# Expert inputs by one-hot tables on TensorE in place of scatters through memory, and another order of modulation, norms and z products in the front

## The chip, the cores and the metric

The kernel runs on one core of a Trainium2 chip. The metric is the device time of one execution in microseconds. A core has TensorE (PE in the profile, with its weight loads as PEld), VectorE (DVE), ScalarE (ACT), GpSimd (POOL) and SyncE (SP); they run side by side, each takes its own instructions in order, and they meet at semaphores. SP and POOL issue DMAs, which all share 16 DMA engines.

## The reference, cut to what matters

Two layers on 1024 tokens of width 256. In each, a conditioning vector c gives six rows (shift, scale and gate for the mixer and for the feed-forward part). Layer 0 is a Mamba-like mixer (SSD) and a mixture of 64 experts, top 8, with room for 64 tokens each; layer 1 is sliding-window attention and a dense feed-forward part with 4-bit weights.

```python
mod = silu(c) @ wmod                      # six rows of 256 per layer
# layer 0, mixer
proj = u_n @ in_proj_w.T                  # z 512, x 512, B 128, C 128, dt 8
B, C = rms_norm(B), rms_norm(C)
dA = softplus(dt + dt_bias) * -exp(A_log)
y = ssd_chunked(x, dA, B, C) + x * D
u = u + (y * silu(z)) @ out_proj_w.T
# layer 0, experts (E 64, K 8, CAP 64, H 256, I 96)
w, sel = top_k(softmax(x @ gate_w.T), K);  w = w / sum(w)
pos = the token's place in its expert's queue;  valid = pos < CAP
xin = zeros((E, CAP + 1, H)).at[eid, slot].set(x[tok])
h = silu(xin @ wg) * (xin @ wu);  out = h @ wd
y[tok] += out[eid, slot] * w
# layer 1: attention (16 heads, window 64), then a gated feed-forward part
vals = NVFP4_LUT[codes] * scales          # weights 3 x 2048 x 256
```

## The kernel before, in words

Rows of tokens are in T = 8 tiles of 128. The order of every engine's work is written out by hand.

**Front.** PE forms the modulation rows with `modulation(n)` (six pieces of 512 columns, three per layer); ACT copies them out with `copy_mod(n)`. Piece 0 comes first. The loop over the tiles then transposes a normalized tile and projects B, C, dt and x; pieces 1 to 5 are put between the tiles of that loop, one in each of five passes. DVE reworks the gate rows (lines 907 to 919) once all six pieces are copied, and only then does the short dt chain to `dA_ready`. PE makes four of the eight z products (`project(..., proj_z)`) while that goes on, then the cumulative sums, `cs_rows(0)`, and the transposes of B and C in pairs of tiles, with one more z product after each pair; a z product waits for a bank that ACT has emptied with a Silu. DVE norms B and C (lines 933 and 934); POOL forms xD (line 372) and xdec (line 376), and scales w_out by the gate (line 380).

**SSD loop.** T + 2 = 10 steps. Step s works on tile s in the scan (PE, with the decay matrices from ACT line 531), on tile s - 1 in the output projection (the residual sum is DVE line 1027), and on tile s - 2 in the router: logits, top 8 (`choose`), and the place in each expert's queue (`place_rows`, DVE lines 991 to 996, which reads a PE product in bank 5). For each of the eight experts of a token POOL issues an indirect DMA (line 392) that writes the token's row of h to its slot in `expert_in` in HBM: 64 of them, each of 128 rows of 1 KB. `expert_in` is 4 MB and is set to zero at the start by one DMA of SP (line 295). After the last tile DVE makes the experts' weights per token (lines 1037 to 1048).

**Groups.** Four experts make a group, g = 0 to 15. POOL reads the group's 256 rows back from `expert_in` (line 399). PE turns them with four transposes in `rows_T` (line 1437), ACT copies them to `xgT` with scale and shift. PE multiplies by gate and up weights (`gate_up`), ACT applies Silu (line 611), DVE multiplies (`hid`, line 1088), PE transposes (line 1459) and multiplies by the down weights, ACT copies out (line 598) and POOL stores to `expert_out` (line 409). PE's order in one pass is `rows_T(g+1)`, `hidden_T(g-1)`, `gate_up(g)`, `down(g-1)`.

SP loads expert weights in pairs of experts (576 KB), 13 buffers deep (NS), 13 pairs before the groups. Between them it loads the 4-bit codes and scales of layer 1 in twelve chunks, `load_codes(n)`: one DMA of codes and eight of scales, from which DVE makes the weights in two halves, `decode(n, par)` (lines 1061 to 1072). A chunk has two buffers, so `load_codes(n)` waits for the decoding of chunk n - 2. The decoding stands in DVE's order between the `hid` products, 1.5 halves per group (PACE), chunk 0 before the first:

```python
while late < 2 * NQ and late < 2 * NEARLY + (g + 1) * PACE:
    decode(late // 2, late % 2)
```

**After the groups** SP loads attention's weights (lines 340 to 348), POOL gathers each token's eight results from `expert_out` (lines 422 and 427), and layer 1 follows. None of that is touched.

Of the kernel before, what the change touches and what calls it, by code (L numbers as in the profile page):

```python
# [8 lines left out]
def adaln_two_layers(nc, x_in, w_in, w_out, gate_w, wgu, wd, wmod, ccol, cols, rows, sinks, rope, consts,  # L9
# [10 lines left out]
    P = 128  # L20
# [8 lines left out]
    xin = nc.dram_tensor("expert_in", (SLOTS, DM), f32, kind="Internal").ap()  # L29
# [3 lines left out]
    with ctx:  # L33
# [24 lines left out]
        def under(v, n):  # L58
# [31 lines left out]
        scatter8 = at(small + 432, T, TOPK).bitcast(u32)  # L90
# [33 lines left out]
        zero = at(A1 + 360, 1024)  # L124
        gabs = at(A0 + 16976, 4, DM)
# [7 lines left out]
        zero_set, xin_zeroed = sem("zero_set"), sem("xin_zeroed")  # L133
# [3 lines left out]
        mod_rest_ready = sem("mod_rest_ready")  # L137
        var_ready, rstd_ready = sem("var_ready"), sem("rstd_ready")
# [12 lines left out]
        NS = 13  # L151
# [4 lines left out]
        NX = 4  # L156
        xg = [at(XB + 5120 + 512 * i, 2, DM) for i in range(2)] + [at(XB + 512 * i, 2, DM) for i in range(2)]
# [17 lines left out]
        mask_ready, pos_mm, place_read, slots_ready, scattered = map(  # L175
            sem, ["mask_ready", "pos_mm", "place_read", "slots_ready", "scattered"])
        wout_ready, cols_mm = sem("wout_ready"), sem("cols_mm")
        w_loaded = [sem(f"w_loaded{i}") for i in range(NS)]
        xg_loaded = [sem(f"xg_loaded{i}") for i in range(NX)]
# [19 lines left out]
        NEARLY, PACE = 1, 1.5  # L199
# [49 lines left out]
        places = [(A0 + 2048 * i, "gu_hi") for i in range(4)] + [(A0 + 8192, None)] + [(B0 + 2048 * i, "low") for i in range(6)] + [  # L249
            (D0, None), (D0 + 1536, "it_low"), (D0 + 3072, "it_hi"), (D0 + 4608, None), (A1, "h4_hi"), (A1 + 1024, None),  # L250
            (X0, "dn_hi"), (X1, "h4_low"), (X1 + 1088, "h4_low"), (X0 + 4224, "dn_hi"), (X0 + 6272, None), (X0 + 8448, "h4_hi"),
            (X0 + 9472, None)]
        split = []
        gap = ctx.enter_context(nc.sbuf_tensor("gap", [P, A0], f32))
# [22 lines left out]
        def _(sp):  # L277
# [16 lines left out]
            sp.wait_ge(zero_set, 1)  # L294
            sp.dma_start(xin.rearrange("(p r a) c -> p r (a c)", p=P, r=8), under(zero, 8)).then_inc(xin_zeroed, 16)
# [25 lines left out]
            for q, tile, early in ((0, 1, True), (1, 2, True), (2, 2, True), (3, 3, True), (6, 3, True), (12, 4, True), (4, 1, False),  # L321
                                   (5, 2, False), (7, 4, False), (8, 5, False), (9, 6, False), (10, 7, False)):
# [3 lines left out]
            load_pair(11)  # L326
# [3 lines left out]
            for g in range(NG):  # L330
                while n < NQ and 2 * (n - 2) < 2 * NEARLY + g * PACE:
                    load_codes(n)
                    n += 1
# [4 lines left out]
                if g == 13:  # L338
                    sp.wait_ge(down_mm, 13)
# [15 lines left out]
        def _(pool):  # L355
            pool.memset(zero, 0.0).then_inc(zero_set, 1)
# [38 lines left out]
            def load_rows(g):  # L395

                if g >= NX:
                    pool.wait_ge(xgT_mm, g - NX + 1)
                pool.dma_start(xg[g % NX], xin[4 * CAP * g:4 * CAP * (g + 1), :].rearrange("(q p) c -> p q c", p=P))\
                    .then_inc(xg_loaded[g % NX], 16)  # L400

            pool.wait_ge(scattered, 16 * T * TOPK)
# [1449 lines left out]
```

## Time and profile before

| | us |
|---|---|
| median of 3 runs (717.51 to 725.04) | 719.66 |
| the profiled execution, its own time | 719.88 |
| its span in the profile | 718.1 |
| PE busy | 563.4 (78%) |
| DVE busy | 444.9 (62%) |
| ACT busy | 307.5 (43%) |
| POOL busy | 260.4 (36%) |

Times in the profile are from the span's start. The mean granted TensorE clock of this execution is 0.894 of full speed. Full is 2.4 GHz; the other level seen is half of it. A TensorE product in plain float32 leaves two records of matmul, one with rounded operands (fp32r) or a transpose leaves one.

### The profile page before, as it was taken

How to read it: one execution, taken by the hardware profiler on the slowest of the kernel's cores; microseconds unless marked ns; L12 is line 12 of the kernel's file. 1: busy time of each engine (PE TensorE's matmuls, PEld its weight loads, DVE VectorE, ACT ScalarE, POOL GpSimd, SP SyncE). 2: the span in 40 equal slices, each digit the busy share in tenths (PEclk: the TensorE clock that was granted, in tenths of full speed). 3: DMA queues.
4: the chain of work that ended last, by engine and by line, in shares of the span. 5: the costliest groups of instructions: out<-in, count | busy, mean ns of one | idle time of the engine just before them, and what ended most of it. 6: DMA issues, size and time to landing. Idle time of an engine off the chain costs nothing.

```text
span 718.1 us, 9581 instructions
## 1 busy us (share of the span) xinstructions
PE 563.4 (78%) x3092; PEld 423.2 (59%) x3092; DVE 444.9 (62%) x981; ACT 307.5 (43%) x951; POOL 260.4 (36%) x305
## 2 busy tenths in 40 slices
PE   2996998596506657476377999999999799998996
PEld 0553676374304434345254777677677688887885
DVE  5729466352398436331688799999786565745444
ACT  2664445242203423232257887887886211111110
POOL 2225507635573311116664554631110355610000
PEclk9899999786557967789687999999999999999999
DMA  8700135331305999882222232330000000000000
GB/s 309 306 1 0 38 128 199 110 104 54 93 0 148 283 310 303 265 306 81 74 58 53 31 50 40 49 41 1 1 1 1 1 0 1 1 8 22 1 1 29
DMA packets 28753, 62.90 MB, mean 88 GB/s; under 512 B 7779, under 2 KB 11025, under 8 KB 28192
## 3 DMA queue, kind: packets, MB, share of 16 engines
q1 hardware_dynamic: 20000, 41.30, 18.3%
q0 software_dynamic: 8704, 21.00, 11.5%
q8 instruction: 25, 0.41, 0.2%
q14 instruction: 24, 0.20, 0.1%
HBM read 48.63 MB, written 17.83 MB: 93 GB/s over the span
## 4 chain that ended last, share of the span: by engine, by line
PE 44%; DVE 24%; issue 10%; DMA 7%; POOL 5%; ACT 4%; another core or an unknown queue 3%; SPq 2%; POOLq 0%; DVEq 0%; ACTq 0%
PE bank L1269 40%; DMA arena<-in_usc 3%; POOL expert_in L392 2%; DVE arena L1099 2%; ACT arena L748 2%; DMA arena<-in_dsc 2%; DVE arena L1195 2%; POOL arena L422 1%; POOL arena L427 1%; SPq L313 1%; DMA arena<-in_wmod 1%; DVE arena L1164 1%; DVE arena L934 1%; DMA expert_out<-arena 1%
## 5 line engine op out<-in xcount | busy, mean ns | idle before, releaser
L1269 PE MATMUL bank<-arena 128*128 128x128 f32 (+9 forms) x1848 | 366.9, 389 | 38.0 <-DMA arena<-in_wmod 8.3
L1269 PEld LDWEIGHTS bank<-arena 128*128 128x128 f32 (+4 forms) x1848 | 249.9, 188 | 122.4 <-issue 76.1
L392 POOL DMA_INDIRECT expert_in<-arena x64 | 65.5, 1024 | 67.3 <-DVE arena L996 46.6
L855 ACT ACTIVATE arena<-bank 128x512 f32<-128x512 f32 x32 | 19.2, 599 | 113.4 <-PE bank L1269 113.4
L1250 DVE TENSOR_TENSOR arena<-arena,bank 128x512 f32<-128x512 f32 x32 | 22.0, 687 | 56.6 <-ACT arena L855 56.6
L1269 PE MATMUL bank<-h_hi,gu_hi 128*128 128x512 f32 x128 | 50.7, 396 | 1.0 <-issue 0.5
L1269 PE MATMUL bank<-h_low,gu_hi 128*128 128x512 f32 x128 | 50.5, 394 | 0.0
L1269 PE MATMUL bank<-h_hi,low 128*128 128x512 f32 x128 | 50.1, 391 | 0.0
L456 POOL TENSOR_TENSOR low<-arena,gu_hi 128x128 fp32r<-128x128 f32 x64 | 29.9, 499 | 55.4 <-DVE dn_hi L1199 55.4
L422 POOL DMA_INDIRECT arena<-expert_out,arena x32 | 37.1, 1160 | 9.2 <-issue 8.4
L1269 PE MATMUL bank<-dn_hi,it_hi 128*128 128x256 f32 x128 | 36.4, 285 | 3.9 <-DVE it_low L1252 3.9
L409 POOL DMA_DIRECT2D expert_out<-arena x16 | 11.6, 726 | 74.9 <-ACT arena L598 74.9
L470 ACT ACTIVATE arena<-arena 128x1 f32<-128x1 f32 (+2 forms) x42 | 13.2, 313 | 56.5 <-DVE arena L872 37.1
L427 POOL DMA_INDIRECT arena<-expert_out,arena x32 | 33.6, 1051 | 8.8 <-issue 8.4
L1269 PE MATMUL bank<-low,it_hi 128*128 128x256 f32 x128 | 36.2, 283 | 0.0
L1269 PE MATMUL bank<-dn_hi,it_low 128*128 128x256 f32 x128 | 36.2, 283 | 0.0
L748 ACT ACTIVATE arena<-bank,arena 128x128 f32<-128x128 f32 x64 | 28.3, 461 | 11.0 <-DVE arena L1169 11.0
L435 POOL TENSOR_TENSOR arena<-arena 128x544 f32<-128x544 f32 x8 | 10.6, 1330 | 59.5 <-ACT arena L664 59.5
L1459 PE MATMUL bank<-arena 128*96 128x128 f32 x32 | 7.3, 315 | 29.4 <-DVE arena L1088 29.4
L1437 PE MATMUL bank<-arena 128*128 128x128 f32 x64 | 11.4, 309 | 23.7 <-DMA arena<-expert_in 23.7
L773 ACT ACTIVATE arena<-bank,arena 128x128 f32<-128x128 f32 x64 | 28.5, 489 | 1.0 <-issue 1.0
L1099 DVE SCALAR_TENSOR_TENSOR arena<-arena 128x256 f32<-128x256 f32 x56 | 27.2, 485 | 2.0
(235 smaller groups left out, 1040.5 us busy)
## 6 DMA issues: line engine op xcount, KB each, us to landing
arena<-in_wgu SPq DMA_DIRECT2D x32, 384.0 KB, 4.8
arena<-in_wd SPq DMA_DIRECT2D x32, 192.0 KB, 6.7
expert_in<-arena SPq DMA_DIRECT2D x1, 4096.0 KB, 23.8
arena<-expert_in POOLq DMA_DIRECT2D x16, 256.0 KB, 7.1
expert_out<-arena POOLq DMA_DIRECT2D x16, 256.0 KB, 7.1
arena<-in_w SPq DMA_DIRECT2D x1, 2048.0 KB, 9.1
arena<-in_wmod SPq DMA_DIRECT2D x1, 1536.0 KB, 15.3
arena<-in_w_in SPq DMA_DIRECT2D x1, 1288.0 KB, 8.9
```

What stands on the lines that cost most here:

```text
L392: pool.indirect_dma_start(xin, bass.IndirectOffsetOnAxis(scatter8[:, t, k:k + 1], 0), h[:, t, :], None, bounds_check=SLOTS - 1, oob_is_err ...
L422: pool.indirect_dma_start(gath[t % 2][:, k, :], None, yex, bass.IndirectOffsetOnAxis(gather8[:, t, k:k + 1], 0), bounds_check=SLOTS - 1, o ...
L427: pool.indirect_dma_start(gath[t % 2][:, k, :], None, yex, bass.IndirectOffsetOnAxis(gather8[:, t, k:k + 1], 0), bounds_check=SLOTS - 1, o ...
L456: pool.tensor_tensor(rounded(w[:, j, cols]), w[:, j, cols], rounded(gu_hi[i][:, a, j]), ALU.subtract)
L470: link(act.activation(o, i, ACT.Ln, bias=eps, scale=scale))
L748: act.activation(Pb[0][:, i, :], o[:, (i % 4) * P:(i % 4 + 1) * P], ACT.Exp, scale=rx[t % 2][:, 0 + i:0 + i + 1], bias=mx[0][:, i:i + 1], ...
L773: act.activation(Pb[1][:, i, :], o[:, (i % 4) * P:(i % 4 + 1) * P], ACT.Exp, scale=rx[t % 2][:, 8 + i:8 + i + 1], bias=mx[1][:, i:i + 1], ...
L855: act.activation(gl[n % 3], bank[2 * (n % 3)][:, :], ACT.Gelu_apprx_tanh).then_inc(gl_ready, 1)
L1099: link(dve.scalar_tensor_tensor(g[:, 0, :], g[:, k, :], w8[:, t, k:k + 1], g[:, 0, :], ALU.mult, ALU.add))
L1195: dve.tensor_tensor(Pb[1], Pb[1], over(den[1], P), ALU.mult).then_inc(pn_ready, 1)
L1250: link(dve.tensor_tensor(it[n % 3], gl[n % 3], bank[2 * (n % 3) + 1][:, :], ALU.mult))
L1269: return pe.matmul(o, lhsT, rhs, start=start, stop=stop, **kw)
```

## The change

1. `expert_in` is gone, with the fill by zero, the 64 scatters and the 16 loads of rows. DVE keeps `negpos` (minus the place of each token in each expert's queue) in `place_rows`, and for every group compares it with a row of numbers (`spots(g)`: four tensor_tensor of 128 x 512, is_equal), which gives a table of ones, tokens by slots. `rows_T(g)` becomes 32 matmuls of 128 x 256 in fp32r that multiply the rows of h by the table. h is split in two rounded halves by POOL first (one copy and one subtraction for each tile, `halves_ready`). Tables are made two groups ahead in two buffers.
2. The tables take memory: NS goes from 13 to 9 pairs. The expert weights of line 1037 to 1048 are made between the first groups, after `hid`. Decoding starts at group 4, two halves a group; `load_codes(n)` is issued from SP's pass n + 1 on. Attention's weights wait for the last `rows_T` and the 14th `down`.
3. In the front, modulation pieces 1 to 5 go behind the loop over the tiles: piece 1 before the cumulative sums, piece 2 after `cs_rows(0)`, pieces 3 to 5 behind the first three pairs of transposes. All eight z products come after the transposes. DVE's gate rework goes behind the norms and transposes' copies, and counts `mod_rest_ready` once for each layer. POOL's xdec waits for all norms and for the last modulation piece.

```diff
@@ SP
-            sp.wait_ge(zero_set, 1)
-            sp.dma_start(xin.rearrange("(p r a) c -> p r (a c)", p=P, r=8), under(zero, 8)).then_inc(xin_zeroed, 16)
...
-                while n < NQ and 2 * (n - 2) < 2 * NEARLY + g * PACE:
+                while n < NQ and n <= g - 1:
                     load_codes(n)
                     n += 1
...
                 if g == 13:
-                    sp.wait_ge(down_mm, 13)
+                    sp.wait_ge(down_mm, 14)
+                    sp.wait_ge(xgT_mm, NG)
@@ POOL
             pool.wait_ge(decs_ready, 3)
+            pool.wait_ge(bcn_ready, 2 * T)
+            pool.wait_ge(mod_mm, 6)
...
-            pool.wait_ge(xin_zeroed, 16)
             for t in range(T):
-                pool.wait_ge(slots_ready, t + 1)
-                for k in range(TOPK):
-                    pool.indirect_dma_start(xin, bass.IndirectOffsetOnAxis(scatter8[:, t, k:k + 1], 0), h[:, t, :], None,
-                                            bounds_check=SLOTS - 1, oob_is_err=False).then_inc(scattered, 16)
...
+                pool.wait_ge(rowsT_mm, T + t + 1)
+                if t >= 4:
+                    pool.wait_ge(st_mm, 4)
+                pool.tensor_copy(rounded(h_hi[t]), h[:, t, :]).then_inc(pool_chain, 1)
+                pool.wait_ge(pool_chain, T + t + 1)
+                pool.tensor_tensor(rounded(h[:, t, :]), h[:, t, :], rounded(h_hi[t]), ALU.subtract).then_inc(halves_ready, 1)
@@ DVE
+                link(dve.tensor_tensor(negpos[:, t, :], slotv[:, t, :], rows_s[:, 24:88], ALU.subtract))
+                dve.max(slot8[:, t, :], slotv[:, t, :])
...
+            def spots(g):
+                if g >= 2:
+                    dve.wait_ge(xgT_mm, g - 1)
+                for i in range(4):
+                    ins = dve.tensor_tensor(rounded(spot[g % 2][:, :, CAP * i:CAP * (i + 1)]), over(negpos[:, :, 4 * g + i], CAP),
+                                            under(minus_c, T), ALU.is_equal)
+                ins.then_inc(spot_ready, 1)
+
+            dve.wait_ge(yT_mm, T)
+            spots(0)
+            spots(1)
...
             for g in range(NG):
+                if g + 2 < NG:
+                    spots(g + 2)
                 dve.wait_ge(sg_ready, g + 1)
                 if g >= 2:
                     dve.wait_ge(hidT_mm, g - 1)
                 up = bank[2 + g % 2][:, 0:4 * FI].rearrange("p (i a f) -> p i a f", i=2, a=2)[:, :, 1, :]
                 dve.tensor_tensor(hid[g % 2], sg[g % 2], up, ALU.mult).then_inc(hid_ready, 1)
-                while late < 2 * NQ and late < 2 * NEARLY + (g + 1) * PACE:
+                if g == 0:
+                    expert_weights()
+                if 1 <= g <= TOPK // 2:
+                    expert_weight(2 * g - 2)
+                    expert_weight(2 * g - 1)
+                while late < 2 * NQ and late < 2 * (g - 3):
                     decode(late // 2, late % 2)
                     late += 1
@@ PE
             def rows_T(g):
-                pe.wait_ge(xg_loaded[g % NX], 16 * (g // NX + 1))
+                pe.wait_ge(spot_ready, g + 1)
                 if g >= 2:
                     pe.wait_ge(xgT_ready, 2 * (g - 1))
-                for q in range(2):
-                    for j in range(KC):
-                        ins = pe.transpose(bank[g % 2][:, (2 * q + j) * P:(2 * q + j + 1) * P], xg[g % NX][:, q, j * P:(j + 1) * P], ident)
+                for j in range(KC):
+                    for t in range(T):
+                        for part in (h_hi[t], h[:, t, :]):
+                            ins = mm(bank[g % 2][:, 2 * P * j:2 * P * (j + 1)], rounded(part[:, j * P:(j + 1) * P]), rounded(spot[g % 2][:, t, :]),
+                                     start=t == 0 and part is h_hi[t], stop=t == T - 1 and part is not h_hi[t])
                 ins.then_inc(xgT_mm, 1)
@@ PE, front
-                if 3 <= s < 8:
-                    if s == 3:
-                        pe.wait_ge(ld_mod_rest, 32)
-                    modulation(s - 2)
-            pe.wait_ge(rowsT_ready, 2 * T)
-            pe.wait_ge(mod_copied, 6)
-            for t in range(4):
-                if t == 3:
-                    pe.wait_ge(xs_ready, T)
-                project(t, bank[(6, 7, 5, 3)[t]], 0, DI, proj_z)
+            pe.wait_ge(ld_mod_rest, 32)
+            modulation(1)
...
             cs_rows(0)
+            pe.wait_ge(rowsT_ready, 2 * T)
+            modulation(2)
+            pe.wait_ge(xs_ready, T)
             for q in range(T // 2):
...
                 ins.then_inc(bcT_mm, 1)
-                t = 4 + q
-                pe.wait_ge(z_ready, t - 3)
-                project(t, bank[(6, 7, 5, 3)[q]], 0, DI, proj_z)
+                if q < 3:
+                    modulation(3 + q)
+            for t in range(T):
+                if 1 <= t < 4:
+                    pe.wait_ge(mod_copied, 3 + t)
+                if t >= 4:
+                    pe.wait_ge(z_ready, t - 3)
+                project(t, bank[Z_BANK[t % 4]], 0, DI, proj_z)
```

## Rows read from the trace of the kernel before

**Rows 1.** Windows: start:end, length, busy PE, PEld, DVE, ACT, POOL; clock, DMA share, GB/s.
```profile
57.00:72.00 15.00, 9.15 (x37) 4.77 (x36) 13.95 (x29) 7.54 (x21) 10.40 (x10) 0.89 0.00 0
235.00:314.00 79.00, 48.74 (x368) 31.66 (x364) 37.76 (x86) 26.79 (x60) 15.18 (x22) 0.78 0.98 288
```

**Rows 2.** Timeline of DVE, line 1027, once per tile: start, length, form, idle before.
```profile
94.14 0.42 DVE L1027 TENSOR_TENSOR arena<-arena,bank 128x256 f32<-128x256 f32 x1 [0.37 <-PE bank L1269]
...
116.55 0.42 DVE L1027 TENSOR_TENSOR arena<-arena,bank 128x256 f32<-128x256 f32 x1 [0.74 <-remote]
126.93 0.42 DVE L1027 TENSOR_TENSOR arena<-arena,bank 128x256 f32<-128x256 f32 x1 [0.31 <-issue]
...
191.44 0.42 DVE L1027 TENSOR_TENSOR arena<-arena,bank 128x256 f32<-128x256 f32 x1 [4.53 <-issue]
```

**Rows 3.** The chain that ended last: its shares by engine, and one piece.
```profile
PE 44%; DVE 24%; issue 10%; DMA 7%; POOL 5%; ACT 4%; another core or an unknown queue 3%; SPq 2%; POOLq 0%; DVEq 0%; ACTq 0%
...
129.38 8.71 another core or an unknown queue
```

**Rows 4.** The page's groups: the scatters, busy and mean ns, idle before.
```profile
L392 POOL DMA_INDIRECT expert_in<-arena x64 | 65.5, 1024 | 67.3 <-DVE arena L996 46.6
```

**Rows 5.** Timeline of the front: POOL's xdec, z products, PE before the loop.
```profile
61.52 7.10 POOL L376 TENSOR_TENSOR arena<-arena 128x512 f32<-128x512 f32 x7 [7.22 <-ACT arena L523]
...
66.86 3.40 PE L1269 MATMUL bank<-arena 128*128 128x512 f32 x4 [3.74 <-ACT arena L540]
...
74.50 1.88 PE L1269 MATMUL bank<-arena 128*128 128x512 f32 x4
...
78.59 0.60 PE L1354 MATMUL bank<-arena 128*128 128x128 f32 x4
```

**Rows 6.** Timeline of PE: one group's round, then fp32r products of layer 1.
```profile
245.21 0.66 PE L1437 MATMUL bank<-arena 128*128 128x128 f32 x4
...
246.02 2.38 PE L1269 MATMUL bank<-arena 128*64 128x192 f32 x24
248.33 0.66 PE L1437 MATMUL bank<-arena 128*128 128x128 f32 x4
...
599.77 0.28 PE L1269 MATMUL bank<-dn_hi,it_hi 128*128 128x256 f32 x1
599.89 0.28 PE L1269 MATMUL bank<-low,it_hi 128*128 128x256 f32 x1
```

**Rows 7.** DVE: expert weights (window as rows 1), halves of a chunk, wide products.
```profile
199.70:220.70 21.00, 0.18 (x1) 0.21 (x2) 20.01 (x33) 0.00 (x0) 15.61 (x16) 0.50 0.12 29
...
220.57 0.42 DVE L1061 TENSOR_SCALAR arena<-arena 128x512 int16<-128x512 int16 x1
222.55 0.43 DVE L1064 TENSOR_SCALAR arena<-arena 128x512 int16<-128x512 int16 x1
...
358.14 0.72 DVE L1148 TENSOR_TENSOR arena<-arena 128x544 f32<-128x544 f32 x1
358.77 0.72 DVE L1149 TENSOR_TENSOR arena<-arena 128x544 f32<-128x544 f32 x1
```

**Rows 8.** Waits of DVE for codes (total, times, longest); code loads in the chain.
```profile
DVE arena L1061 <- DMA arena<-in_usc: 18.0, 4, 8.0
...
236.96 0.65 SPq L311
...
241.52 7.07 DMA arena<-in_usc
...
257.02 13.04 DMA arena<-in_usc
```

**Rows 9.** Timeline of DVE: the last place read, first and last hid.
```profile
198.89 0.21 DVE L992 TENSOR_TENSOR arena<-arena,bank 128x64 f32<-128x64 f32 x1
...
225.41 0.35 DVE L1088 TENSOR_TENSOR arena<-arena,bank 128x192 f32<-128x192 f32 x1 [0.92 <-ACT arena L611]
...
313.13 0.35 DVE L1088 TENSOR_TENSOR arena<-arena,bank 128x192 f32<-128x192 f32 x1 [0.48 <-ACT arena L611]
```

More of the change, by code:

```diff
@@ L89, in adaln_two_layers @@
         gather8 = at(small + 368, T, TOPK).bitcast(u32)
-        scatter8 = at(small + 432, T, TOPK).bitcast(u32)
+        minus_c = at(small + 900, CAP)
         h2_cols = at(small + 498, 2 * KC)
@@ L123, in adaln_two_layers @@
         nA = at(A1 + 352, H)
-        zero = at(A1 + 360, 1024)
-        gabs = at(A0 + 16976, 4, DM)
+        gabs = at(A0 + 21712, 2, DM)
         X0 = A1 + 1392
@@ L155, in adaln_two_layers @@
         wd_s = [at(o + 4 * KC * FI, 2, DM, parts=FI) for o in slot_at]
-        NX = 4
-        xg = [at(XB + 5120 + 512 * i, 2, DM) for i in range(2)] + [at(XB + 512 * i, 2, DM) for i in range(2)]
+        h_hi = [at((A1 + 360, XB + 5120)[t // 4] + DM * (t % 4), DM) for t in range(T)]
+        spot = [at(A0 + 7168 + 2048 * i, T, 2 * P) for i in range(2)]
+        negpos = at(XB, T, E)
         xgT = [at(XB + 1024 + 512 * i, 4, P) for i in range(2)]
@@ L319, in load_codes @@
                                      blocks[r:r + 1, 2 * c:2 * c + 2, :].to_broadcast([16, 2, DM])).then_inc(pk_loaded[i], 16)
[L321 to L322 removed]
+            for q, tile, early in ((0, 1, True), (1, 2, True), (2, 2, True), (3, 3, True), (6, 3, True), (4, 1, False),
+                                   (5, 2, False), (7, 4, False), (8, 5, False)):
                 sp.wait_ge(st_mm if early else yT_mm, tile)
@@ L410, in _ @@
                     .then_inc(ob_stored[g % 3], 16)
+            for g in range(NG):
+                store_rows(g)
             for i in range(3):
@@ L535, in _ @@
             decay_matrices(0)
+            for n in range(2, 6):
+                copy_mod(n)
             act.wait_ge(L_ready, 1)
@@ L539, in _ @@
                 act.wait_ge(proj_z, t + 1)
-                act.activation(zs[:, t, :], bank[(6, 7, 5, 3)[t % 4]][:, :], ACT.Silu).then_inc(z_ready, 1)
+                act.activation(zs[:, t, :], bank[Z_BANK[t % 4]][:, :], ACT.Silu).then_inc(z_ready, 1)
             act.wait_ge(z_ready, T)
@@ L951, in _ @@
                 dve.tensor_scalar(cT[:, 2 * q:2 * q + 2, :], both[:, 1], wbc, None, ALU.mult).then_inc(bcT_ready, 1)
+            dve.wait_ge(mod_copied, 6)
+            for i in range(2):
+                for j in (1, 4):
+                    if i or j == 4:
+                        dve.tensor_scalar(mod[i][:, j, :], mod[i][:, j, :], 1.0, None, ALU.add)
+                    g, a = mod[i][:, j + 1, :], gabs[:, j // 4, :]
+                    link(dve.scalar_tensor_tensor(a, g, -1.0, g, ALU.mult, ALU.max))
+                    link(dve.tensor_scalar(a, a, 0.25, None, ALU.max))
+                    link(dve.tensor_scalar(g, g, 0.0, 2.0, ALU.is_ge, ALU.mult))
+                    ins = dve.scalar_tensor_tensor(g, g, -1.0, a, ALU.add, ALU.mult)
+                    if j == 4:
+                        ins.then_inc(mod_rest_ready, 1)
+                    else:
+                        link(ins)
             hd = lambda v: v.rearrange("p (a b) -> p a b", b=HD)
@@ L1000, in _ @@
             dve.memset(run_b[:, 0, :], 0.0)
+            dve.tensor_scalar(minus_c, rows_s[:, 24:88], -NOWHERE, 1.0 / CAP, ALU.add, ALU.mult)
             make_M(0)
@@ L1035, in _, with expert_weights, expert_weight @@
                     normed(h[:, t, :], x[:, t, :], t, mv[2], rstd[2]).then_inc(h2_ready, 1)
-            link(dve.tensor_tensor(eqk, prob, mask_b, ALU.mult))
-            link(dve.tensor_reduce(rsum, eqk, AX, ALU.add))
-            dve.reciprocal(rsum, rsum)
-            link(dve.tensor_tensor(wvalid, wvalid, prob, ALU.mult))
-            link(dve.tensor_tensor(wvalid, wvalid, over(rsum, E), ALU.mult))
-            link(dve.tensor_scalar(eqk[:, :, 0:TOPK], slot8, -1.0, NOWHERE, ALU.mult, ALU.add))
-            link(dve.tensor_scalar(gather8, eqk[:, :, 0:TOPK], float(SLOTS - 1), None, ALU.min))
-            for k in range(TOPK):
+            def spots(g):
[8 more added lines that the diff above has]
+            spots(1)
+            def expert_weights():
+                link(dve.tensor_tensor(eqk, prob, mask_b, ALU.mult))
+                link(dve.tensor_reduce(rsum, eqk, AX, ALU.add))
+                dve.reciprocal(rsum, rsum)
+                link(dve.tensor_tensor(wvalid, wvalid, prob, ALU.mult))
+                link(dve.tensor_tensor(wvalid, wvalid, over(rsum, E), ALU.mult))
+                link(dve.tensor_scalar(eqk[:, :, 0:TOPK], slot8, -1.0, NOWHERE, ALU.mult, ALU.add))
+                link(dve.tensor_scalar(gather8, eqk[:, :, 0:TOPK], float(SLOTS - 1), None, ALU.min))
+            def expert_weight(k):
                 link(dve.tensor_tensor(eqk, slotv, over(slot8[:, :, k], E), ALU.is_equal))
@@ L1472, in _ @@
             pe.wait_ge(place_read, T)
+            pe.wait_ge(halves_ready, T)
             rows_T(0)
```

68 lines of the change are left out of this document (20 added, 48 removed).

## The prediction, made before the changed kernel was run

> **What bounds the kernel now.** I read the chain of waits first, then the timelines of the stretches that it passes through, then windows over them. The change touches three: the front up to PE's work at 78.59 [rows 5], the SSD loop from there to the last place read at 198.89, and the groups up to the last hid at 313.13 [rows 9]. What follows is the same work in the same order.
>
> In the front PE is the bound, except between 57 and 72, where it works 9.15 of 15 us [rows 1]: it waits 3.74 us for ACT's Silu copies, and its next z products take 3.40 us where others take 1.88 [rows 5].
>
> In the SSD loop a step is bound by the exchange between PE and DVE. Line 1027 runs once per step. Two neighbours are 126.93 - 116.55 = 10.4 us apart; from the first to the last, seven steps, it is 191.44 - 94.14 = 97.3 us, 13.9 each [rows 2]. The rest is pauses: 3% of the chain, 21.5 us, is put down to an unknown queue, and one piece of it is 8.71 us long [rows 3]. All pieces of over 1 us lie between 112 and 176, while scatters are issued. In the pauses PE, DVE and ACT stand still together, and PE's clock falls afterwards.
>
> After the loop POOL still works off its scatters: 64 of 1.02 us, with small gaps 1.3 apart, are 82 us of POOL [rows 4], and the rows have to come back. The first hid is 225.41 - 198.89 = 26.5 us behind the last place read.
>
> In the groups two things bound together. The DMA engines are 98% busy at 288 GB/s [rows 1]. DVE waits for codes, 18.0 us in four waits for one kind of scales [rows 8], and hid is queued behind the decoding, so PE waits too. An undisturbed round of PE is 248.33 - 245.21 = 3.1 us [rows 6], while the sixteen groups take 313.13 - 225.41 = 87.7 us [rows 9], 5.8 each.
>
> **The change part by part.**
>
> *Front.* PE's work stays the same. The order removes its idle time: 15 - 9.15 = 5.85 us [rows 1], and 3.40 - 1.88 = 1.5 us of slow products [rows 5], together 7.4 at best. Piece 1 of the modulation covers the dt chain of DVE and ACT. POOL's xdec, 7.1 us [rows 5], starts later, but then has the time of eight z products, about 14 us at 1.88 less overlap [rows 5], as cover; DVE's gate rework lies under the same z products, and if that cover is too short, the first M product is late by the rest. I take 6.5 of the 7.4; the bounds are 0 and 7.4. Term: **-6.5**.
>
> *SSD loop.* 64 scatters go. POOL gets two operations of 256 columns per tile instead; one of 512 takes it 7.10 / 7 = 1.0 us [rows 5], so they need less than 2.1 us of a step of 10.4: hidden. DVE's one small added operation replaces another. If the pauses come from the scatters, seven steps cost 7 x 10.4 = 72.8 instead of 97.3 [rows 2]. Term: **-24.5**; the other bound is 0. I take the first because the step from 116.55 to 126.93 shows that the work needs no more, and because the chain has such pauses nowhere but among the scatters.
>
> Here a rule of the Trainium skill speaks against the obvious mechanism, late instructions: the page "Runtime: NRT & Kernel Launch", section "Instruction fetch mechanics", says that each sequencer fetches its next block by a DMA queue of its own and that crossing a block is mostly hidden. By that rule the pauses would have another cause than a fetch delayed by the scatters, and this term could be 0. The trace does not name the cause, so this is the first rival.
>
> *From the last place read to the first hid.* The wait for scatters and rows goes. New on this path: slots, about 1 us of small operations as 0.21 us each [rows 9]; four table products of DVE. Products 544 wide start 358.77 - 358.14 = 0.63 apart [rows 7], so spots(0) is about 2.5 us (2.9 if they don't overlap, at 0.72). Then rows_T(0) and rows_T(1): fp32r products of 256 columns start 0.12 apart [rows 6], so 32 are 3.84 us and both 7.7; PE has been idle and at half clock after the loop (0.50 in [rows 7]), which I price at 3.8 for the first. gate_up is 16 of the 24 records in 2.38 us [rows 6], 1.6, and Silu 0.6 behind it; copies are hidden. Sum 1 + 2.5 + 7.7 + 3.8 + 1.6 = 16.6, against 26.5. Term: **-9.9**, between -13 (full clock) and -6 (half for both).
>
> *Groups.* PE's round grows: 3.1 - 0.4 + 3.84 = 6.5 us, as the transposes cost 0.4 up to hidden_T. DVE per group: tables 2.5, hid 0.4, and a chunk twice 222.55 - 220.57 = 1.98, 4.0 [rows 7]: 6.9. So DVE sets the pace in the groups that decode, and PE is just behind. From first to last hid DVE has: the expert weights, which were free before because they lay under the scatters, 20.9 us [rows 7]; 13 tables, 32.5; 15 hid, 6; 11 chunks (the last comes behind hid(15)), 43.6. Sum 103.0, against 15 x 6.5 = 98 for PE. Handing over between two engines so close costs something: I add 3. The table for g + 2 is made before hid(g), so it delays hid(g) only if DVE is late; it waits for rows_T(g), which is done by then. 103 + 3 = 106.
>
> The codes: their load waits for the decoding two chunks back. The nine DMAs take 241.52 - 236.96 = 4.6 us of SP's queue, and the pair loads stand behind them. With a landing L after the last issue, two rounds of DVE cannot be shorter than 4.6 + L + 4.0. Landings seen are 7.07 and 13.04 [rows 8], with the DMA engines full. At 7.07 that is 7.8 a group, 0.9 over 6.9. But the traffic falls: 23 pairs of 0.59 MB, 12 chunks of 0.52 and 16 stores of 0.26 are 24 MB in 106 us, 227 GB/s, against 288. I take 3 us in all, between 0 and 43 (L = 13.04: 10.8 a group, 11 times 3.9). Groups: 109 against 87.7. Term: **+21.3**. NS = 9 still leaves four groups of weights in hand.
>
> *Behind the groups.* Attention's weights wait one step longer, but their load started 6 us ahead of the last hid before and starts about 5 ahead now; POOL's last stores and gathers keep their distance to the last hid. Term 0, at most +3. The fill by zero lay under the front: 0.
>
> Sum: -6.5 - 24.5 - 9.9 + 21.3 = **-19.6**. From the profiled 719.88 (span 718.1) that is **700.3 us**. The median, 719.66, is 0.2 lower; I keep 700.
>
> **Rivals.**
>
> *A. The pauses stay.* They belong to something that the change leaves alone, a fetch of instructions or the weight loads. For it: the cause is unnamed, and instruction blocks are fetched in that time too. Against: the steps before the scatters run the same code on PE and have no such pause. The loop's term is 0: 700 + 24.5 = 725. If half of them stay, 712.
>
> *B. Slower: the code loads set the pace.* SP issues nine DMAs per chunk behind pair loads, decoding is now two halves a group, and every hid stands behind it. At L = 13.04 the groups take 40 us more: 740. It decides from the point where a group takes 1.8 us more than forecast (19.6 / 11), L about 10; 727 is reached at 2.4 more. For: the chain before goes through exactly these loads. Against: the traffic of `expert_in` is gone and a round is longer.
>
> *C. Better.* PE at full clock from the start, no wait for codes, a step nearer to the 10 us: about 690.
>
> **Chances.** Forecast 0.57 (own range 692 to 711), A whole 0.13, A half 0.10, B 0.14, C 0.06. No change can be told from a change within 1%, that is 712.5 to 726.9. Faster: forecast, C and half of "A half": 0.68. Same: A, the other half, and a small part of B: 0.19. Slower: most of B, 0.13. Range 686 to 727: it takes in C, the forecast and A and leaves out most of B.
>
> **What would show it.** In the changed profile: no scatter and no pause of an unknown queue in the SSD loop, with line 1027's successor every 10.4 us; PE's first work of the loop near 72; about 16.6 us from the last place read to the first hid; from first to last hid about 109 us, DVE busy more than 90% there, table products 0.63 apart, and PE's clock full. The prediction is wrong if DVE waits for codes over 10 us in all, if pauses of several us with every engine still remain, or if rows_T takes much over 3.84 us.

## The result, and the profile after

The changed kernel takes **700.14 us** in the median of four runs (698.35 to 704.53), where the kernel before took 721.98 on the same chip (717.51 to 725.04). The ratio is 0.9711, with a 95% interval from 0.9653 to 0.977. The profiled execution of the changed kernel took 699.33 us with a span of 697.7, so its stages can be summed against the 718.1 of before.

| stage of the profiled span | before | after | difference | forecast |
|---|---|---|---|---|
| start to the first residual sum | 94.1 | 92.2 | -2.0 | -6.5 |
| seven steps of the SSD loop | 97.3 | 73.2 | -24.1 | -24.5 |
| last step to the last place read | 7.5 | 7.5 | 0 | 0 |
| last place read to first hid | 26.5 | 15.1 | -11.4 | -9.9 |
| first to last hid | 87.7 | 106.5 | +18.8 | +21.3 |
| behind the last hid | 405.0 | 403.3 | -1.7 | 0 |
| sum | 718.1 | 697.7 | -20.4 | -19.6 |

**The SSD loop** first. This is DVE's timeline in the changed kernel: the line that adds the residual, once per tile, with start, length, form, and the idle time before it. It answers to [rows 2].

```profile
92.16 0.42 DVE L1020 TENSOR_TENSOR arena<-arena,bank 128x256 f32<-128x256 f32 x1 [0.37 <-PE bank L1286]
102.25 0.42 DVE L1020 TENSOR_TENSOR arena<-arena,bank 128x256 f32<-128x256 f32 x1 [0.54 <-PE bank L1286]
112.67 0.42 DVE L1020 TENSOR_TENSOR arena<-arena,bank 128x256 f32<-128x256 f32 x1 [0.54 <-PE bank L1286]
...
165.34 0.42 DVE L1020 TENSOR_TENSOR arena<-arena,bank 128x256 f32<-128x256 f32 x1 [4.35 <-PE bank L1286]
```

Every step takes 10.1 to 10.8 us; 165.34 - 92.16 is 73.2 for seven. The shares of the chain by engine answer to [rows 3]: the unknown queue has gone from 3% to 0%.

```profile
PE 51%; DVE 31%; issue 5%; ACT 5%; DMA 4%; SPq 3%; another core or an unknown queue 0%; DVEq 0%; ACTq 0%
```

**The front** gave less than its term. The timeline of POOL, PE and DVE there, which answers to [rows 5] (lines 934 to 939 are the gate rework, 951 is an M product, DVE's table of decays times the scores):

```profile
57.59 7.55 POOL L374 TENSOR_TENSOR arena<-arena 128x512 f32<-128x512 f32 x7 [11.68 <-PE bank L1286]
57.69 14.12 PE L1286 MATMUL bank<-arena 128*128 128x512 f32 x34
...
59.95 1.02 DVE L937 TENSOR_SCALAR arena<-arena 128x256 f32<-128x256 f32 x1
...
65.46 0.29 DVE L937 TENSOR_SCALAR arena<-arena 128x256 f32<-128x256 f32 x1
...
71.65 0.60 PE L1371 MATMUL bank<-arena 128*128 128x128 f32 x4
...
74.76 0.90 DVE L939 SCALAR_TENSOR_TENSOR arena<-arena 128x256 f32<-128x256 f32 x1
76.21 1.21 DVE L951 TENSOR_TENSOR arena<-arena,bank 128x1024 f32<-128x1024 f32 x1
77.48 0.96 PE L1286 MATMUL bank<-arena 128*128 128x128 f32 x3 [3.01 <-DVE arena L951]
```

PE runs through its products without a gap and begins the loop's transposes at 71.65, 6.9 us ahead of the 78.59 of before. But line 951, DVE's first M product, stands behind the gate rework. The rework's small operations (line 937) take 1.02 us beside POOL's xdec and 0.29 in a gap of POOL's work, so DVE is not through before 75.66, and PE idles 3.01 us. In the kernel before, the same nineteen operations ran from 50.54 to 58.15. The clock is granted at 0.91 from 72 to 92.

**Behind the loop and in the groups**: DVE's last place read, the first tables, two products of rows_T(0) and the first and last hid. They answer to [rows 9].

```profile
172.84 0.21 DVE L984 TENSOR_TENSOR arena<-arena,bank 128x64 f32<-128x64 f32 x1
173.75 4.89 DVE L1034 TENSOR_TENSOR spot<-arena 128x512 fp32r<-128x512 f32 x8
...
177.15 0.41 PE L1286 MATMUL bank<-spot,h 128*128 128x256 f32 x1
177.36 0.41 PE L1286 MATMUL bank<-spot,h_hi 128*128 128x256 f32 x1
...
187.96 0.35 DVE L1100 TENSOR_TENSOR arena<-arena,bank 128x192 f32<-128x192 f32 x1 [3.11 <-ACT arena L602]
...
294.44 0.35 DVE L1100 TENSOR_TENSOR arena<-arena,bank 128x192 f32<-128x192 f32 x1 [1.58 <-ACT arena L602]
```

Tables take 0.61 us each, and the first products of 256 columns start 0.21 apart, at half clock. Windows over the front, and from the first table product over two parts of the groups (columns as in [rows 1]) show what became busy:

```profile
57.00:72.00 15.00, 15.00 (x43) 7.09 (x42) 13.73 (x17) 6.43 (x10) 12.77 (x12) 1.00 0.00 0
72.00:92.00 20.00, 16.99 (x98) 12.85 (x97) 11.71 (x17) 8.00 (x27) 9.03 (x13) 0.91 0.27 89
177.00:230.00 53.00, 47.47 (x387) 42.19 (x387) 44.83 (x81) 13.45 (x30) 3.87 (x5) 0.92 0.39 119
230.00:295.00 65.00, 61.97 (x529) 52.02 (x530) 55.84 (x115) 20.53 (x47) 6.53 (x9) 0.95 0.97 279
```

PE's busy share in the groups rises from 62% [rows 1] to 90% and 95%. DVE's waits from 180 to 300 (total, times, longest) answer to [rows 8]: the code loads, which had cost 18.0 us for one kind of scales, cost 2.9 now. The wait of 3.7 lies before the first hid.

```profile
DVE arena L1100 <- ACT arena L602: 8.3, 4, 3.1
DVE spot L1034 <- PE bank L1286: 3.7, 1, 3.7
DVE arena L1071 <- DMA arena<-in_dsc: 2.9, 4, 1.0
```

### The profile page after: what moved, and what is told of

It reads as the page before. It is cut to its first block, busy times and chain, and to the rows that moved or that the text cites. A ratio compares the mean times of both kernels' runs of the same rounds, so it can differ in the third digit from the quotient of the medians.

```text
span 697.7 us, 10429 instructions
## 1 busy us (share of the span) xinstructions
PE 605.5 (87%) x3540; PEld 472.3 (68%) x3540; DVE 485.9 (70%) x1046; ACT 307.0 (44%) x951; POOL 193.2 (28%) x240
## 4 chain that ended last, share of the span: by engine, by line
PE 51%; DVE 31%; issue 5%; ACT 5%; DMA 4%; SPq 3%; another core or an unknown queue 0%; DVEq 0%; ACTq 0%
PE bank L1286 48%; DVE spot L1034 3%; DMA arena<-in_w 2%; ACT arena L739 2%; DVE arena L1212 2%; DVE arena L1116 1%; SPq L315 1%; ACT arena L764 1%; DMA arena<-in_wmod 1%; DVE arena L1124 1%; DMA arena<-in_dsc 1%; DVE arena L936 1%; DVE arena L1054 1%; DVE arena L1055 1%; DVE arena L1053 1%
## 5 line engine op out<-in xcount | busy, mean ns | idle before, releaser
L1286 PE MATMUL bank<-arena 128*128 128x128 f32 (+9 forms) x1848 | 355.1, 377 | 32.3 <-DMA arena<-in_wmod 8.3
L1286 PEld LDWEIGHTS bank<-arena 128*128 128x128 f32 (+4 forms) x1848 | 241.6, 182 | 114.4 <-issue 73.1
L1286 PE MATMUL bank<-spot,h_hi 128*128 128x256 f32 x256 | 67.1, 300 | 9.5 <-DVE spot L1034 9.4
L1286 PE MATMUL bank<-spot,h 128*128 128x256 f32 x256 | 65.3, 293 | 0.0
L1286 PEld LDWEIGHTS bank<-spot,h_hi 128*128 128x128 f32 x256 | 51.6, 202 | 15.3 <-DVE spot L1034 10.8
L1286 PEld LDWEIGHTS bank<-spot,h 128*128 128x128 f32 x256 | 51.5, 201 | 0.0
L576 ACT ACTIVATE arena<-bank,arena 128x256 f32<-128x256 f32 x32 | 16.3, 560 | 68.9 <-PE bank L1286 68.9
L1286 PE MATMUL bank<-h_hi,gu_hi 128*128 128x512 f32 x112 | 44.4, 397 | 1.0 <-issue 0.5
L1034 DVE TENSOR_TENSOR spot<-arena 128x512 fp32r<-128x512 f32 x64 | 39.8, 684 | 3.9 <-PE bank L1286 3.7
L446 POOL TENSOR_TENSOR low<-arena,gu_hi 128x128 fp32r<-128x128 f32 x56 | 26.5, 504 | 50.4 <-DVE dn_hi L1216 50.4
L739 ACT ACTIVATE arena<-bank,arena 128x128 f32<-128x128 f32 x64 | 28.3, 460 | 9.6 <-DVE arena L1186 9.6
## 6 DMA issues: line engine op xcount, KB each, us to landing
arena<-in_w SPq DMA_DIRECT2D x1, 2048.0 KB, 10.4
```

The costliest lines, as they stand in the source:

```text
L446: pool.tensor_tensor(rounded(w[:, j, cols]), w[:, j, cols], rounded(gu_hi[i][:, a, j]), ALU.subtract)
L576: act.activation(by_chunk[:, j], bank[g % 2][:, 2 * P * j:2 * P * (j + 1)].rearrange("p (q c) -> p q c", q=2), ACT.Identity, scale=h2_cols ...
L739: act.activation(Pb[0][:, i, :], o[:, (i % 4) * P:(i % 4 + 1) * P], ACT.Exp, scale=rx[t % 2][:, 0 + i:0 + i + 1], bias=mx[0][:, i:i + 1], ...
L1034: ins = dve.tensor_tensor(rounded(spot[g % 2][:, :, CAP * i:CAP * (i + 1)]), over(negpos[:, :, 4 * g + i], CAP), under(minus_c, T), ALU.is ...
L1286: return pe.matmul(o, lhsT, rhs, start=start, stop=stop, **kw)
```

## Experiments

The stages of every profiled run, in us. "Choice" is the last search for the eight best slots, 0.5 us behind the last place read in the kernel before and 0.8 in the changed one.

| kernel | first residual | seven steps | last choice to first hid | first to last hid | behind | median, ratio to before |
|---|---|---|---|---|---|---|
| before | 94.1 | 97.3 | 26.0 | 87.7 | 405.0 | |
| after | 92.2 | 73.2 | 14.4 | 106.5 | 403.3 | 700.1, 0.971 |
| after again | 91.4 | 72.9 | 14.2 | 104.0 | 406.3 | 702.6, 0.977 |
| no scatter | 97.3 | 73.4 | 24.9 | 89.8 | 404.7 | 698.6, 0.966 |
| no bytes | 94.2 | 88.2 | 26.4 | 86.6 | 404.7 | 720.3, 0.999 |
| direct | 97.2 | 73.4 | 24.9 | 88.3 | 405.1 | 700.7, 0.971 |
| front alone | 90.4 | 94.3 | 27.2 | 88.0 | 405.5 | 716.6, 0.997 |
| after + scatters | 91.0 | 92.5 | 14.2 | 105.9 | 406.0 | 716.3, 0.999 |
| rework late | 87.0 | 74.1 | 14.5 | 106.2 | 407.8 | 698.5, 0.971 |
| weights late | 92.6 | 74.1 | 14.1 | 98.0 | 405.6 | 692.2, 0.962 |
| both late | 87.9 | 72.9 | 14.0 | 99.7 | 405.4 | 690.5, 0.960 |
| short decode | 91.8 | 73.4 | 14.1 | 100.6 | 406.2 | 697.1, 0.972 |
| half rows | 91.7 | 74.9 | 11.2 | 105.1 | 405.0 | 695.1, 0.969 |

### What makes the pauses of the SSD loop

**No scatter.** The kernel before, without

```diff
-                for k in range(TOPK):
-                    pool.indirect_dma_start(xin, ..., h[:, t, :], None, ...).then_inc(scattered, 16)
...
-            pool.wait_ge(scattered, 16 * T * TOPK)
```

> The kernel before without its 64 scatters and without the wait for them: expert_in stays zero, so the experts work on zeros; all other work is the same. Main theory (the pauses of PE, DVE and ACT in the SSD loop come from the scatters): the seven steps between the line that adds the residual take 73 us instead of 97, no wait on an unknown queue is left there, and from the last place read to the first hid it is under 10 us, since neither POOL's tail nor the rows' return is waited for: about 720 - 24 - 18 = 678 us. Rival (the pauses belong to instruction fetches or weight loads that the change leaves alone): only the tail goes, 720 - 18 = 702 us, and the loop stays at 97 us.

The seven steps took 73.4 us, as the theory says; the rival's 97 is out. The whole came to 698.6 us (ratio 0.9659, 0.9578 to 0.974), not 678: the first hid was hardly nearer, where the expectation had it under 10 us behind the last place read. The window from the last choice to it shows why: DVE is busy 23.78 of 25.00 us.

```profile
178.40:203.40 25.00, 5.04 (x28) 3.66 (x28) 23.78 (x42) 3.28 (x7) 3.86 (x5) 0.57 0.16 52
```

The expert weights (20 us of DVE [rows 7]) and the first decoding stand there. POOL's tail had covered them, and I had left my own row out of that expectation. Its first residual, and that of "direct" below, came 3 us late, in a stretch of the front (72 to 80) where the clock was granted at 0.63 instead of 1.00.

**No bytes.** The kernel before, with all places out of bounds: every scatter is issued, nothing is written.

```diff
-                dve.tensor_scalar(scatter8[:, t, :], slot8[:, t, :], -1.0, NOWHERE, ALU.mult, ALU.add)...
+                dve.tensor_scalar(scatter8[:, t, :], slot8[:, t, :], 0.0, NOWHERE, ALU.mult, ALU.add)...
```

> The kernel before with every scatter issued, but with all its places out of bounds, so that POOL works off the same 64 instructions and no row is written (expert_in stays zero). If POOL's work on the indirect form causes the pauses, the loop stays near 97 us and the scatters near 1.0 us each, and the time is 715 to 720 us. If the written bytes cause them, the loop falls to about 73 us and the time to about 690 us; the tail of POOL behind the last place read stays in both.

720.3 us in ten runs, ratio 0.9987 (0.9943 to 1.0031). The profiled run took 88.2 us for seven steps, with six waits on an unknown queue of 1.4 to 4.6 us in its chain; the two longest are shown. Its own time, 709.8, is the shortest of its ten runs (709.8 to 725.5 us). The written bytes are not needed for the pauses. Whether they lengthen them is not told by one trace. The kernel before says the same by itself: from 161.5 to 193 us POOL issues 18 scatters, its DMA queue moves only 0.41 MB, and a pause of 6.69 us lies there.

```profile
151.13 3.94 another core or an unknown queue
...
164.74 4.62 another core or an unknown queue
```

**Direct.** The kernel before, with 64 times 128 KB written by direct DMAs of POOL into blocks of fixed place (the experts then read rows that are not theirs). These are not the same bytes, as the expectation has it, but twice as many: by the DMA queues' sums the direct DMAs move 8.4 MB and the scatters 4.2, since the experts have room for 4096 rows of the 8192.

```diff
...
-                    pool.indirect_dma_start(xin, ..., h[:, t, :], None, ...).then_inc(scattered, 16)
+                    r = TOPK * t + k
+                    pool.dma_start(xall[P * r:P * (r + 1), :], h[:, t, :]).then_inc(scattered, 16)
```

> The kernel before with each scatter replaced by a direct DMA that POOL issues, same bytes (a 128-row tile of h into DRAM at a fixed place). If the indirect form causes the pauses, the loop takes about 73 us; POOL's issue is shorter, so the tail shrinks too: 680 to 695 us. If the written bytes or any DMA of POOL cause them, the loop stays at 85 to 97 us and the time is 705 to 720 us.

700.7 us, ratio 0.9709 (0.963 to 0.9787), seven steps in 73.4 us and no wait of an unknown queue in the loop. The window over the seven steps, and then its timeline around one residual sum:

```profile
97.20:170.60 73.40, 65.41 (x365) 48.90 (x368) 44.05 (x133) 34.66 (x130) 25.90 (x48) 0.93 0.52 170
```

```profile
109.97 4.52 POOL L394 DMA_DIRECT2D expert_in<-arena  x8 [26.96 <-DVE arena L997]
117.66 0.42 DVE L1028 TENSOR_TENSOR arena<-arena,bank 128x256 f32<-128x256 f32 x1 [0.54 <-PE bank L1270]
120.04 4.28 POOL L394 DMA_DIRECT2D expert_in<-arena  x8 [5.55 <-DVE arena L997]
```

The DMA engines move 170 GB/s in this loop, and nobody pauses. So it is the indirect form on POOL, neither the traffic nor the fact that POOL issues DMAs. The direct DMAs are also shorter on POOL (0.54 us each, 0.98 for an indirect one), and no run here makes the two equally long.

**After + scatters.** The changed kernel with 48 scatters (tiles 0 to 5, rows of x) behind the halves; nothing reads what they write.

```diff
+                if t < 6:
+                    pool.wait_ge(slots_ready, t + 1)
+                    for k in range(TOPK):
+                        pool.indirect_dma_start(xin, ..., x[:, t, :], None, ...).then_inc(scattered, 16)
...
```

> The changed kernel with 48 scatters put back into the SSD loop: for tiles 0 to 5, POOL scatters rows of x by the slots behind the two halves, and they are waited for only before the gathers; nothing reads what they write. Theory (POOL's indirect DMAs cause the pauses, whatever the code around them): wait pieces of 2 to 9 us on an unknown queue come back, the seven steps take 85 to 97 us instead of 73, the whole 712 to 724 us. Rival (the pauses came from where the old code's instruction blocks lay): 73 to 75 us and 700 to 703 us.

716.3 us in ten runs, ratio to before 0.9987 (0.9952 to 1.0023): the whole gain is gone. Seven steps took 92.5 us, and the pauses are back in other code. A part of its timeline:

```profile
119.95 0.98 POOL L399 DMA_INDIRECT expert_in<-arena  x1 [0.30 <-issue]
120.39 0.73 ACT L571 ACTIVATE arena<-bank 128x512 f32<-128x512 f32 x1
121.17 4.35 PE L1296 MATMUL bank<-arena 128*128 128x256 f32 x28 [0.34 <-ACT arena L571]
121.23 0.98 POOL L399 DMA_INDIRECT expert_in<-arena  x1 [0.30 <-issue]
...
126.11 0.69 DVE L1021 TENSOR_TENSOR arena<-arena,bank 128x512 f32<-128x512 f32 x1 [5.17 <-remote]
```

POOL goes on at 1.28 us a scatter while DVE waits 5.17 us for something that no queue of the profile accounts for; in the changed kernel the same operation (its line 1011) never waits over 1.6 us. The same is to be seen in the kernel before, in the pause of 8.71 us of [rows 3]: the product for which DVE's line 968 waits is over by 131.8 at the latest, and DVE starts at 138.12. ACT, which waits for the transposes in front of that product, is late too, and POOL never stops.

```profile
129.70 2.11 PE L1269 MATMUL bank<-arena 128*128 128x128 f32 x6
...
134.53 0.81 ACT L552 ACTIVATE arena<-bank,arena 128x128 f32<-128x128 f32 x2 [5.94 <-remote]
...
138.01 0.98 POOL L392 DMA_INDIRECT expert_in<-arena  x1 [0.30 <-issue]
138.12 0.69 DVE L968 TENSOR_TENSOR arena<-arena 128x512 f32<-128x512 f32 x1 [8.74 <-remote]
```

Two explanations can be put aside from the traces. Late instructions: no packet of an instruction queue moves from 128 to 160 us or from 161.5 to 193 in the kernel before, though pauses of 8.71, 2.80 and 6.69 us lie there; in the changed kernel six such packets fall between the first and the last residual sum, and every step takes its 10.1 to 10.8 us. And POOL's scatters do not slow DVE's own work: behind the loop, beside the last scatters, an operation of the expert weights takes what it takes in the changed kernel without scatters (0.69 us). It is what waits for another engine that comes late.

```profile
207.65 0.69 DVE L1046 TENSOR_TENSOR arena<-arena 128x512 f32<-128x512 f32 x1
```

### The front

**Front alone.** The kernel before with the third part of the change, as it stands in the diff ahead, and its scatters kept.

> The kernel before with the third part of the change alone: the other order of modulation, norms and z products in the front, scatters kept. By the trace of the changed kernel: the transposes that open PE's work of the loop start at about 72 instead of 78.6, the first M of DVE is late, and the line that adds the first residual starts at about 92 instead of 94.1, so 2 us less, 718 us. By the prediction (a term of -6.5 that is handed on): 713 us. If the pauses of the loop depend on where instruction blocks are crossed and not on the scatters, they may move by several us in either direction.

716.6 us in ten runs, ratio 0.997 (0.9929 to 1.001): at most 5 us, perhaps nothing. The first residual came at 90.4, 3.7 us earlier; its clock was 1.00 from 72 to 92, where the changed kernel had 0.91 and 92.2. The pauses stayed (94.3 us for seven steps), so the new order of the front is not what removes them.

**Rework late.** The changed kernel, with layer 1's half of the gate rework in the step s == T of the loop.

```diff
-            dve.wait_ge(mod_copied, 6)
-            for i in range(2):
+            def rework(i):
                 for j in (1, 4):
...
+            dve.wait_ge(mod_copied, 6)
+            rework(0)
...
                 if 0 <= s - 2:
                     choose(s - 2)
+                if s == T:
+                    rework(1)
```

> The changed kernel with layer 1's half of the gate rework (eight small DVE operations and one more) taken out of the front and put into a step of the SSD loop where DVE is idle for 4.3 us. Theory: the rework, beside POOL's xdec, makes the first M product late by 3.0 us of idle PE and some slow products, so the first residual comes about 4 us earlier (88 instead of 92.2) and the time is 696 us. Rival: M waits for something else in the front (the last Silu copy, POOL's xdec), then nothing moves: 700 us.

The mechanism is as said, with ten operations moved. DVE's first M product starts at 72.37 instead of 76.21, PE runs on without the 3.01 us of idle time, and the first residual is at 87.0.

```profile
71.85 8.32 PE L1290 MATMUL bank<-arena 128*128 128x128 f32 x57
...
72.37 1.21 DVE L953 TENSOR_TENSOR arena<-arena,bank 128x1024 f32<-128x1024 f32 x1
```

The time follows less surely: 698.5 us (696.1 to 700.5) against 702.6 (698.6 to 704.4) for the changed kernel on the same chip, but the intervals of the two ratios overlap (0.9652 to 0.9758, 0.9714 to 0.9819). Its profiled execution and the one of the changed kernel run again lie 0.9 us apart in span: the 4.4 us of the front were gone by the end, 1.2 in the loop, 2.1 in the groups and 1.5 behind them.

### The groups

**After again.** No edit.

> The changed kernel once more, on the chip of the next three, as their base. Seen so far: 700.1 us (698.4 to 704.5); 699 to 701 expected.

702.6 us, a little above the expectation. Its trace has 104.0 us of groups and 406.3 behind them, where the first had 106.5 and 403.3: single stages move by 2 to 3 us from run to run.

**Weights late.** The changed kernel, with the eight expert weights behind the groups (their inputs are kept in three tiles of their own).

```diff
-                if 1 <= g <= TOPK // 2:
-                    expert_weight(2 * g - 2)
-                    expert_weight(2 * g - 1)
...
+            for k in range(TOPK):
+                expert_weight(k)
```

> The changed kernel with the eight expert weights (24 operations of 0.69 us, 17 us of DVE) moved from the groups to behind them, where DVE waits for the gathers. Theory (DVE's sum sets the length of the groups, 103 us of work in 106.5): first to last hid falls to PE's 15 x 6.5 = 98 to 100 us, 692 to 694 us in all. Rival (PE's rounds of 6.5 and its waits for weights set it and DVE is only beside it): 105 to 107 us, 699 to 701 us. Rival (the code loads set the pace): the waits for codes grow by what DVE gives free.

692.2 us, ratio 0.9622 (0.9564 to 0.9679), and 98.0 us from first to last hid, which is 15 times PE's 6.53. This is the changed kernel around the fourth group with weights: DVE's hid, PE's next group, and a round where nothing but decoding stands.

```profile
215.12 0.34 DVE L1100 TENSOR_TENSOR arena<-arena,bank 128x192 f32<-128x192 f32 x1
...
225.86 0.34 DVE L1100 TENSOR_TENSOR arena<-arena,bank 128x192 f32<-128x192 f32 x1
225.99 0.58 PE L1286 MATMUL bank<-spot,h_hi 128*128 128x256 f32 x1 [4.14 <-DVE spot L1034]
...
234.72 0.35 DVE L1100 TENSOR_TENSOR arena<-arena,bank 128x192 f32<-128x192 f32 x1 [2.27 <-ACT arena L602]
...
241.24 0.35 DVE L1100 TENSOR_TENSOR arena<-arena,bank 128x192 f32<-128x192 f32 x1
```

Here a round is the time from one hid to the next. A round with decoding alone takes 241.24 - 234.72 = 6.52 us. The round with weights and decoding takes 10.74, PE idles 4.14 in it and comes back at half clock (0.51 granted from 226.0 to 231.9), and so the next round takes 8.86. With the weights away every round stands near 6.5:

```profile
214.89 0.35 DVE L1102 TENSOR_TENSOR arena<-arena,bank 128x192 f32<-128x192 f32 x1 [3.76 <-ACT arena L603]
221.42 0.35 DVE L1102 TENSOR_TENSOR arena<-arena,bank 128x192 f32<-128x192 f32 x1
227.95 0.35 DVE L1102 TENSOR_TENSOR arena<-arena,bank 128x192 f32<-128x192 f32 x1
```

**Both late.** The last two edits together.

> Both moves, that of the rework and that of the expert weights, in one kernel. If both theories hold and the gains add, 688 to 690 us; if the front's gain is taken back behind the loop, 692 to 694 us; if neither holds, 700 us.

690.5 us (689.2 to 692.8), ratio 0.9603 (0.9552 to 0.9653): the lowest of all, 30 us under the kernel before and 10 to 12 under the changed one. Against "weights late" its interval overlaps, so the front's share is not shown.

**Short decode.** The changed kernel, with three of the four operations of each decoding left out.

```diff
...
-                    dve.tensor_scalar(v, codes, 0x7, 9, ALU.bitwise_and, ALU.logical_shift_left)
-                    link(dve.tensor_scalar(s, codes, 0x8, 12, ALU.bitwise_and, ALU.logical_shift_left))
...
-                link(dve.tensor_tensor(f, v, s, ALU.bitwise_or))
...
```

> The changed kernel with three of the four operations of each decoding left out (the codes are scaled as they are, so the experts' weights are wrong); loads and tables stay. DVE's work from the first to the last hid falls by 22 x 1.29 = 28 us, to about 75. Theory: the groups are then PE's, 15 x 6.5 = 98 us, the whole 691 us. Rival (PE or the loads set it already): 105 to 107 us, 699 us. If the loads come to the front when DVE is short, the waits for the scales grow beyond 2.2 us.

697.1 us (ratio 0.972, 0.966 to 0.9779), not told apart from the changed kernel in time, and 100.6 us of groups instead of 104 to 106.5. DVE had about 26 us less to do (70.3 us busy from first to last hid instead of 96.2), and the groups became only 3 to 6 us shorter. Nearly all of that is the round with weights and decoding (8.23 instead of 10.74) and the next one (6.27 instead of 8.86); the rounds with decoding alone were at PE's 6.5 before, and stay there, and DVE now waits 2.4 us in each. The waits for scales did not grow.

```profile
255.31 0.35 DVE L1092 TENSOR_TENSOR arena<-arena,bank 128x192 f32<-128x192 f32 x1 [2.43 <-ACT arena L602]
261.84 0.35 DVE L1092 TENSOR_TENSOR arena<-arena,bank 128x192 f32<-128x192 f32 x1 [2.44 <-ACT arena L602]
```

**Half rows.** The changed kernel, with h_hi alone in the products with the tables.

```diff
-                        for part in (h_hi[t], h[:, t, :]):
+                        for part in (h_hi[t],):
...
```

> The changed kernel with one half of h alone in the products with the tables (16 instead of 32 per group; the low half is missing from the experts' input). PE's round falls from 6.5 to about 4.6 us, DVE's work stays. Theory (DVE sets the pace in the groups): first to last hid falls only to about 103 us, and the first hid comes 2 to 3 us earlier, as rows_T of two groups lies on the path there: 694 us. Rival (PE sets the pace): 15 x 1.9 = 29 us less, 670 us.

695.1 us (ratio 0.9687, 0.9628 to 0.9747), with 105.1 us of groups: half of PE's table products are gone, and PE now waits 18.9 us for tables and 9.1 for weights instead (total, times, longest). The rounds with decoding alone still take 6.5 us, which here is DVE's. The rival's 670 is out. The first hid came 3 us nearer, as said.

```profile
PE bank L1286 <- DVE spot L1034: 18.9, 12, 6.0
PE bank L1286 <- DMA arena<-in_wd: 9.1, 7, 2.7
```

## Why the prediction was right

*The forecast of 700.0 was met to 0.2 us, and its sum of -19.6 came out as -20.4. One term was off by 4.5, three others by 1.5 to 2.5 on the other side, so part of the closeness is luck; the changed kernel run again took 702.6.*

**SSD loop (-24.5, measured -24.1).** Right, and the step of 10.4 us taken from one undisturbed pair of rows held for all seven. The prediction could not name the cause; it argued from where the pauses stood. The experiments name it: take the scatters away or make them direct, and 73 us remain; put 48 into the changed kernel, and 92.5 come back. Rival A is out. How an indirect DMA on POOL delays other engines stays open: no record shows what they wait for.

On the rule of the Trainium skill, "Runtime: NRT & Kernel Launch", section "Instruction fetch mechanics" (crossing into a new block of instructions is mostly hidden): the traces agree. The larger of the two instruction queues carries 25 packets in the kernel before and 29 in the changed one, whose loop has no pause. That the pauses had another cause than a fetch holds too, as no such packet moves in the stretches with the longest of them; but the cause lay in what the change removes, so the term was whole and not 0.

**Last place read to first hid (-9.9, measured -11.4).** Right within its bounds. Tables 0.61 apart, and 0.21 between the products only until 180.6: that costs (0.21 - 0.12) / 0.21 of 4.2 us, 1.8, where 3.8 had been allowed. "No scatter" adds what the prediction had only half seen: with the scatters away and the weights left in place the first hid came only 1.1 us sooner, since DVE's weights and decoding fill the same 25 us. So the gain needs the weights moved; that it needs the tail gone as well is argued, as the weights were not moved alone. The weights were paid for in the groups.

**Groups (+21.3, measured +18.8).** The total was met by two misses that offset each other: DVE was busy 96.2 us and not 103, and stood idle 10.3 and not the 6 allowed for handing over and codes. The code loads stayed harmless (2.9 us of waits; rival B is out), and the DMA engines moved the 227 GB/s that the prediction had worked out. (The landing from which rival B decides was given as about 10 us; by the prediction's own formula 8.7 to 9.0 us a group are 8.8 to 9.3.) But "DVE sets the pace in the groups that decode" was mis-sized. DVE's round there is 2.41 for tables, 0.27 for hid and 3.84 for a chunk, 6.52 us by start to start, not 6.9, and PE's is the same 6.53. DVE is over it only in the groups with expert weights: three rounds of 7.02, one of 10.74 and its echo of 8.86, some 8 us together. "Weights late", "short decode" and "half rows" show the three sides of it: 17 us of DVE taken from those rounds are worth 6 to 8.5, 26 us taken mostly from balanced rounds 3 to 6, and 28 us of PE (16 products of 0.118 in 15 groups) nothing that shows.

**Front (-6.5, measured -2.0).** The step that failed. PE's gain was there (-6.9 at the loop's first work, -6.0 in the changed kernel run again), but "DVE's gate rework lies under the same z products" was not so: 19 operations, several of 1.0 to 1.3 us and one of 2.6, beside POOL's xdec and the work behind it need from 58.6 to 75.7, 17 us where they had taken 7.6. The prediction named what would follow, a late first M product, but gave it no price of its own; only 0.9 of the 7.4 was held back. It cost 3.0 us of idle PE in both traces of the changed kernel, and lower clock some 2 more in the first alone: run again, the kernel had 1.00 from 72 to 92. "Rework late" has the idle time away and the first residual 7.1 us sooner than before, which is the forecast's size.

**Behind the groups (0, measured -1.7).** No effect: the changed kernel run again gave +1.3.

## What to carry to other kernels

Take the undisturbed step of a loop from its quietest pair of rows and price the rest as one cause; then ask which engine is doing something else only while the pauses last. Before an idle stretch is counted as a gain, sum what other engines have to do in it. When work is moved into a loop, put it where that engine waits: 17 us of the same operations cost 6 to 8.5 us inside the groups and nothing that shows behind them.

## What the runs showed of the hardware

- Indirect DMAs issued on POOL make other engines see finished work late, by 1.4 to 8.7 us at a time and 15 to 24 us over 64 of them, even where no byte is written; direct DMAs of POOL with twice the bytes do not. The mechanism stays open. The one such wait in the chain of the changed kernel, 2.96 us at 320.75, stands among its indirect gathers.
- Small DVE operations on 128x256 f32 took 1.02 us beside POOL's elementwise work on 128x512 and 0.29 in a gap of it, in the same line.
- PE came back from 4.14 us without work at half clock, so a stall in one round cost another 2.3 us in the next.
